# Six layers of local attention on one core: which projections stand next to each other in a slot, and how the other engines' orders follow

## What is computed

```python
qkv = shift_tokens(x) @ Wqkv            # 128 x 128 times 128 x 3072
q, k, v = split(qkv, 3)                 # 16 heads of 64 each
q, k = l2norm(q) * qs, l2norm(k) * ks   # norms over each head
q = q * cos * scale + rotate_half(q) * sin * scale     # k with 1 / scale
sim = 8 * q @ k.T                       # windows of 32, looking one window back
out = softmax(mask(sim)) @ v
x = out @ Wo + x
```

## Time and profile before

| | us |
|---|---|
| median of 3 runs (1913.93 to 1918.66) | 1914.29 |
| the profiled execution, its own time | 1919.0 |
| its span, first to last instruction | 1916.2 |

### The profile page before, as it was taken

How to read it: one execution, slowest core, us unless ns; L and a number is a source line. 1 busy time by engine, 2 the same in 40 slices (tenths; PEclk the granted TensorE clock), 3 DMA queues, 4 the chain that set the end, 5 groups by cost and what they waited for, 6 DMA issues and landing times.

```text
span 1916.2 us, 85177 instructions
## 1 busy us (share of the span) xinstructions
PE 1742.9 (91%) x33584; PEld 1377.8 (72%) x33584; DVE 1613.1 (84%) x3868; ACT 1389.4 (73%) x3701; POOL 1331.6 (69%) x1226
## 2 busy tenths in 40 slices
PE   5888869999899999899998899998999998999997
PEld 3444447787777787777787777787787776787776
DVE  6666679999679999589998699996799995899985
ACT  4677657877677877577886677885777875777875
POOL 4444457888478888388887488885688874888882
PEclk9899879999999999999999999999999999999999
DMA  5000011111021111021111211111211110211111
GB/s 130 5 5 4 2 59 42 33 38 40 24 74 41 33 40 39 23 75 40 33 37 32 67 41 40 33 37 31 68 43 38 33 43 20 76 40 39 33 36 48
DMA packets 59087, 77.46 MB, mean 40 GB/s; under 512 B 16608, under 2 KB 31674, under 8 KB 57914
## 3 DMA queue, kind: packets, MB, share of 16 engines
q1 hardware_dynamic: 58938, 75.36, 15.1%
HBM read 22.63 MB, written 1.05 MB: 12 GB/s over the span
## 4 chain that ended last, share of the span: by engine, by line
PE 59%; DVE 14%; ACT 9%; POOL 8%; issue 8%; SPq 1%; DMA 0%; POOLq 0%; DVEq 0%; ACTq 0%
PE y_ps L524 9%; PE s_ps L476 7%; PE proj_ps L455 7%; PE tr_ps L465 6%; POOL qk L1519 5%; PE pv_ps L506 4%; PE proj_ps L457 4%; PE proj_ps L456 4%; ACT square L818 4%; DVE by_cos L1091 3%; PE s_ps L698 3%; DVE by_sin L1091 3%; DVE sumsq L1103 3%; PE y_ps L516 2%; PE proj_ps L684 2%
## 5 line engine op out<-in xcount | busy, mean ns | idle before, releaser
L1512 POOL TENSOR_TENSOR qk<-by_cos,by_sin 128x512 f32<-128x512 f32 x388 | 498.4, 1285 | 199.1 <-DVE by_sin L1091 198.0
L1519 POOL TENSOR_TENSOR qk<-qk,inv_norm 128x512 f32<-128x512 f32 x388 | 404.4, 1043 | 82.2 <-ACT inv_norm L824 67.9
L818 ACT ACTIVATE square<-proj_ps 128x512 f32<-128x512 f32 x364 | 217.6, 598 | 110.0 <-PE proj_ps L457 92.9
L455 PE MATMUL proj_ps<-w_hi,x_hi 128*128 128x512 f32 x546 | 268.2, 491 | 22.9 <-DVE by_sin L1091 20.3
L1091 DVE TENSOR_TENSOR by_cos<-proj_ps,tab 128x512 f32<-128x512 f32 x364 | 249.9, 687 | 34.4 <-ACT square L818 32.5
L465 PE MATMUL tr_ps<-ident,qk 128*128 128x128 f32 x1544 | 238.7, 277 | 40.2 <-POOL qk L1519 25.5
L1103 DVE TENSOR_REDUCE sumsq<-square 128x8 f32<-128x512 f32 x388 | 262.3, 676 | 0.0
L465 PEld LDWEIGHTS tr_ps<-ident,qk 128*128 128x128 f32 x1544 | 181.1, 142 | 110.3 <-POOL qk L1519 79.1
L1091 DVE TENSOR_TENSOR by_sin<-proj_ps,tab 128x512 f32<-128x512 f32 x364 | 247.8, 681 | 0.0
L1525 POOL TENSOR_TENSOR s_sb<-s_sb,row_max 128x512 f32<-128x512 f32 x192 | 205.0, 1068 | 32.5 <-DVE row_max L1122 31.7
L457 PE MATMUL proj_ps<-w_hi,x_lo 128*128 128x512 f32 x546 | 217.1, 398 | 0.0
(11 more groups left out here) (173 smaller groups left out, 4160.5 us busy)
## 6 DMA issues: line engine op xcount, KB each, us to landing
arena<-v SPq DMA_DIRECT2D x388, 130.0 KB, 2.4
w_raw<-in_L_ffn_Wqkv SPq DMA_DIRECT2D x7, 1536.0 KB, 6.8
wo<-in_L_ffn_Wo SPq DMA_DIRECT2D x7, 512.0 KB, 3.9
w_raw<-in_L_ffn_W SPq DMA_DIRECT2D x7, 341.0 KB, 6.2
c_in<-in_ctx SPq DMA_DIRECT2D x16, 64.0 KB, 1.8
xn<-in_fside_BxS SPq DMA_DIRECT2D x1, 1024.0 KB, 6.1
out<-z SPq DMA_DIRECT2D x4, 256.0 KB, 2.9
w<-in_L_ffn_W SPq DMA_DIRECT2D x12, 64.0 KB
```

The source lines that it names most:

```text
L455: pe.matmul(ps[:], x_hi[:], w_hi[:, col], start=True, stop=False)
L818: act.activation(square[:, c % 2, :], ps[QK_AT[c] % 2][:], ACT.Square).then_inc(squared, 1)
L1512: pool.tensor_tensor(heads(qk[:, c, :]), heads(by_cos[:, c % 2, :]), heads(by_sin[:, c % 2, :])[:, :, ::-1, :], ALU.add).then_inc(qk_added, 1)
L1519: pool.tensor_tensor(ap, ap, inv_norm[:, c, :].unsqueeze(2).to_broadcast([128, 8, DH]), ALU.mult).then_inc(qk_ready, 1)
```

## The change

Only the order of calls within a slot changes, on PE, ACT, DVE and POOL. No instruction is added or removed. The core of the diff, in the order PE, ACT, DVE, POOL:

```diff
                     if front_on:
                         project(T + 1, 0)
+                        project(T + 1, 1)
                     if behind >= 1:
                         p_transpose(T - 1, 1)
-                    if front_on:
-                        project(T + 1, 1)
+                    if behind >= 2:
+                        shift_state(T - 2, tile_of(z, n - 2, D // 2))
                     if first:
                         qk_transpose(T, 2)
                     qk_transpose(T, 3)
-                    if behind >= 2:
-                        shift_state(T - 2, tile_of(z, n - 2, D // 2))
                     if behind >= 1:
                         values(T - 1, 1 - par, 1)
-                    if front_on:
-                        project(T + 1, 2)
-                    if behind >= 1:
-                        att_transpose(T - 1, 0)
                     scores(T, par, 1)
...
+                    if behind >= 1:
+                        att_transpose(T - 1, 0)
                     if front_on:
+                        project(T + 1, 2)
                         project(T + 1, 3)
+                        project(T + 1, 4)
                         qk_transpose(T + 1, 0)
+                    p_transpose(T, 0)
                     if behind >= 1:
                         att_transpose(T - 1, 1)
-                    p_transpose(T, 0)
                     if front_on:
-                        project(T + 1, 4)
                         qk_transpose(T + 1, 1)
                         project(T + 1, 5)
...
-                    if front_on:
-                        square_chunk(T + 1, 1)
                     if first:
                         qk_out(T, par, 2)
                     qk_out(T, par, 3)
                     if front_on:
+                        square_chunk(T + 1, 1)
                         norms(T + 1, 0)
-                    if behind >= 1:
-                        att_out(T - 1, 0)
-                    if front_on:
-                        v_out(T + 1, 1 - par, 0)
                     exps(T, 0)
...
                     if front_on:
+                        v_out(T + 1, 1 - par, 0)
+                        norms(T + 1, 1)
                         square_chunk(T + 1, 2)
-                        norms(T + 1, 1)
+                    if behind >= 1:
+                        att_out(T - 1, 0)
...
                     if behind >= 1:
                         sums_inverse(T - 1, 1)
+                        normalise(T - 1, 1)
                     if behind >= 2:
                         dve.wait_ge(stat_done, T - 1)
-                    if behind >= 1:
-                        normalise(T - 1, 1)
+                    if front_on and not last_front:
+                        stage(T + 2, n + 2, L * 4 + 12)
                     if behind >= 2:
                         ln_variance(T - 2, par)
                     if front_on:
-                        clamp_norm(T + 1, 1)
+                        times_cos(T + 1, 2, L - 1)
+                        times_sin(T + 1, 2, L - 1)
+                        sum_squares(T + 1, 2)
                     mask(T, 1)
...
-                    if front_on:
-                        sum_squares(T + 1, 2)
-                    if front_on and not last_front:
-                        stage(T + 2, n + 2, L * 4 + 12)
-                    if front_on:
-                        clamp_norm(T + 1, 2)
-                    if behind >= 2:
-                        ln_apply(T - 2, n - 2, par)
+                    sums_inverse(T, 0)
+                    normalise(T, 0)
                     if front_on:
                         times_cos(T + 1, 3, L - 1)
                         sum_squares(T + 1, 3)
+                        clamp_norm(T + 1, 3)
                         times_sin(T + 1, 3, L - 1)
-                        clamp_norm(T + 1, 3)
-                    sums_inverse(T, 0)
-                    normalise(T, 0)
+                    if behind >= 2:
+                        ln_apply(T - 2, n - 2, par)
...
                         add_rotated(T + 1, 2)
+                        scale_rotated(T + 1, 2)
                     center(T, 1)
                     if not front_on:
                         w_rest(1, L * 3 + 2)
-                    if front_on:
-                        scale_rotated(T + 1, 2)
```

More of the change, by code:

```diff
@@ L999, in slot @@
                     if front_on:
+                        v_out(T + 1, 1 - par, 0)
+                        norms(T + 1, 1)
                         square_chunk(T + 1, 2)
-                        norms(T + 1, 1)
+                    if behind >= 1:
+                        att_out(T - 1, 0)
+                    if front_on:
                         qk_out(T + 1, 1 - par, 0)
+                    p_out(T, 0)
                     if behind >= 1:
@@ L1006, in slot @@
                         ln_std(T - 2, par)
-                    p_out(T, 0)
                     if front_on:
                         qk_out(T + 1, 1 - par, 1)
+                        norms(T + 1, 2)
                         square_chunk(T + 1, 3)
-                        norms(T + 1, 2)
                     if front_on and not last_front:
@@ L1015, in slot @@
                         v_out(T + 1, 1 - par, 1)
+                        qk_out(T + 1, 1 - par, 2)
                     exps(T, 1)
-                    if front_on:
-                        qk_out(T + 1, 1 - par, 2)
                 layer_slots(act.Fori, L, slot)
@@ L1383, in slot @@
                         times_sin(T + 1, 0, L - 1)
-                        clamp_norm(T + 1, 0)
                     if behind >= 2:
@@ L1387, in slot @@
                     if front_on:
+                        clamp_norm(T + 1, 0)
                         times_cos(T + 1, 1, L - 1)
@@ L1390, in slot @@
                         sum_squares(T + 1, 1)
+                        clamp_norm(T + 1, 1)
                     if behind >= 1:
                         sums_inverse(T - 1, 1)
+                        normalise(T - 1, 1)
                     if behind >= 2:
                         dve.wait_ge(stat_done, T - 1)
-                    if behind >= 1:
-                        normalise(T - 1, 1)
+                    if front_on and not last_front:
+                        stage(T + 2, n + 2, L * 4 + 12)
                     if behind >= 2:
@@ L1404, in slot @@
                     if front_on:
-                        times_cos(T + 1, 2, L - 1)
-                        times_sin(T + 1, 2, L - 1)
+                        clamp_norm(T + 1, 2)
                     row_maxima(T, 1)
```

## The result

The changed kernel takes 1969.51 us (median of 4 runs, 1965.38 to 1975.19) against 1916.47 (4 runs, 1913.93 to 1918.81), a ratio of 1.0279 with a 95% interval of 1.0257 to 1.03. It is slower by about 53 us. The profiled executions have spans of 1973.4 and 1916.2, 57.2 apart.

What follows compares the result with a forecast made beforehand. DVE, with 13.92 us of work in a 14.41 us slot, was to bound: +0.32 +0.12 +0.37 +0.12 gives 14.85, above PE's 14.06. Over 78 slots that is 34 us, less 2, so 1946 us (own range 1925 to 1970, widened to begin at 1893).

Steps and rivals of the forecast that it cites:

- The sum of the slot: DVE's work per slot: 13.92 us now plus four terms, 14.85 us after the change.
- Term 1: DVE's ln_apply, moved behind times_sin of chunk 3, stands behind POOL's add: 1.44 us against 1.12, +0.32 per slot.
- The rival in which it gets through: ln_apply's second half asks before POOL's add and costs 0.39 us; PE's 14.06 then bounds, 1885 us; chance 0.18.
- Term 2: DVE's staging, moved behind normalise of T - 1, stands behind POOL's add of chunk 1: 0.47 us against 0.35, +0.12.
- Term 3: DVE's clamps of chunks 1 and 3 wait for their own sums of squares: +0.37 us per slot in all.
- Term 4: DVE's sums_inverse of half 0, now ahead of chunk 3's rotation, waits for the late values: +0.12 us per slot.
- The step of PE's neighbours: Three of six projections per slot directly follow another, first matmul 0.39 us instead of 0.50: 0.3 us saved on PE.
- The size in microseconds: 0.44 us more in each of 78 slots, 34 us, less 2 for slots 0 and 1: 1914.3 + 32 = 1946.

Runs made afterwards that it cites:

- e3: The changed kernel with ln_apply directly behind normalise of half 0, in front of the whole rotation of chunk 3; the slot is longer by 0.60 us.
- e10: The kernel before with projection 1 directly behind projection 0 on PE and p_transpose behind both; 1924.5 us.
- e7: The kernel before with POOL's center of half 1 held back until ln_apply is done; slower by 0.3 to 0.7%.
- e12: The changed kernel without the second half of ln_apply, so part of the result is not computed; 1918.9 us, slot 14.20 us.
- e11: The changed kernel with project 2 on PE between the values of T - 1 and the scores of half 1; 1954.6 us.
- e8: The changed kernel with PE's order of the kernel before, other engines keeping their changed orders; 2048 us.
- e1: The changed kernel with POOL's add_rotated of chunk 3 waiting until ln_apply is done; 0.12 us of the time saved on DVE reaches the slot.
- e2: The changed kernel with ln_apply moved in front of times_sin of chunk 3; 0.18 us of the time saved on DVE reaches the slot.
- e4: The kernel before with ln_apply alone moved behind times_sin of chunk 3; slower by 0.63 us per slot, 49 us in 78.
- e9: The changed kernel with chunk 3's rotation before sums_inverse and normalise, ln_apply before its times_sin, and POOL's center of half 1 waiting for ln_apply; slot 15.15 us.
- e5: The changed kernel with POOL's add_rotated of chunk 3 waiting for ln_apply and ACT's square of chunk 1 at its old place; slot 14.74 us.

## Why the prediction was right, and what it missed

**The sum of the slot held.** Forecast 14.85 us, measured 14.86.

- Term 1: `ln_apply` costs 955.36 - 953.91 = 1.45, forecast 1.44, with the first half through in 0.27 and the second standing, 0.03 us behind POOL, as the earlier trace rows had it. (At 483.85 in those rows the second half lasted 1.07; it did not lose 1.07, as the prediction says. Nothing hangs on that.) By the Trainium skill (SBUF — State Buffer, Who interferes with whom) whoever issues first holds the shared pair for the whole instruction; the traces agree at margins of 0.03 and 0.04 us (954.07 and 954.10 here, 954.04 and 954.08 in e3). The rival in which it gets through is refuted for this place.
- Term 2: the staging takes 0.61 (947.09 to 947.70) and 0.58 in the other slot of the body (961.99 to 962.57), forecast 0.47. +0.25 instead of +0.12. DVE reaches it 3.89 us behind `times_sin` of chunk 0 (943.20), not 4.03, and POOL's add ends 4.49 behind it (forecast 4.50), so it stands longer.
- Term 3: the clamps were too dear. Two now wait for their sum (0.71 behind its start at 945.45 against 0.60), 0.11 each, 0.22 where 0.37 stood.
- Term 4: the wait for the values is 951.06 - 950.27 - 0.60 = 0.19, forecast 0.12.
- Together 0.33 + 0.25 + 0.17 + 0.19 = 0.94, and 13.92 + 0.94 = 14.86. The 0.17 for the clamps is what the other three leave; counted directly it is 0.2. Errors of 0.1 in both directions cancelled.

**The step of PE's neighbours held in size and bought nothing.** Two of three pairs have the short first matmul, the third waits 0.27 for its bank. e10 shows the pair alone at no gain.

**What failed is the picture of the limits behind the sum.** The prediction took a slot for the larger of two amounts, DVE's own work and PE's own sequence. It said that in the kernel before DVE "carries 13.92 us of work in a slot of 14.41", and for the changed kernel it set DVE's 14.85 against PE's 14.06. But the chain of the kernel before is a loop over PE, ACT, DVE and POOL of 14.41 us with 1.89 us of DVE in it, and e7, which took 0.73 us off DVE, gained nothing. That DVE's work and this loop are nearly of one length is chance, and it let the forecast from DVE's work come out. In the changed kernel, too, the chain leaves DVE in each slot: from the rotation of chunk 0 over POOL (944.04) to PE's transposes (948.87) and values, and back to `sums_inverse` at 951.06, where DVE waits 0.19. Term 4 had this wait as 0.12 us of DVE's time, not as the closing of a loop. The rival "The second half gets through" gave 14.06 us and 1885. e12, the nearest to it, gave 14.20 and 1918.9: 0.14 us in 78 slots are 11 us, and slots 0 to 3 and 14 are 17 us longer than before (446.3 against 429.5).

**The size in microseconds was short by 23 us** (1946 against 1969.5). The result lies 0.5 us inside the upper end of the range, and two of its four executions lie above 1970; that it is inside is luck. The step is "so many slots times the difference, 2 us less for slots 0 and 1, nothing for the rest". The 60 slots 4 to 13 gave 29.1, near the forecast (60 x 0.44 = 26). The 30 others gave 30.6, where the prediction had 18 x 0.44 - 2 = 6. Slots 0 and 1 were forecast 2 us shorter and came out 11.4 longer, 3.7 of it without any stall; why these two are slower without `ln_apply`, no run shows. e11 shows that the place of the scores directly behind the values, 64 small matmuls in a row (its expectation counts 96, by the records of the one and the matmuls of the other), causes a large part: project 2 between them takes 15 us off. e8, with PE's old order, has no more stalls than before. That PE is short of instructions there is the reading that fits (small matmuls in a row, code run for the first time); the profile shows only that it waits for nothing else. Why e11 keeps 5.0 us, and what makes the clock fall behind one stall and not behind another, stays open.

**Is the stall the cause of the 53 us?** Of the longer slot, yes. e12 leaves out the stalled half, and the slot falls from 14.86 to 14.20, below the 14.38 of before. e1 and e2 look as if they spoke against it, since the changed kernel still loses 45 us in them; but they buy the missing stall by delaying POOL's add, and the loop of 14.7 us that then holds them has this delay in it. The remaining part, some 18 us, is PE's stalls and what follows them in the slots outside the pattern, and e12 still has it: it gains 11 us against before in the 60 slots 4 to 13 (851.9 against 862.7) and loses 17 in the 30 others. In the kernel before, moving `ln_apply` alone (e4) costs 48 us, by the stall and the lost cover together. No experiment gave a kernel faster than before.

## What to carry to other kernels

- A busy share near the slot's length on one engine doesn't show that this engine binds. Follow the chain of the profile once around a slot and add up the pieces to the slot's length; then look for the second loop before pricing what the first one's removal gives.
- The same stalled instruction is free in front of a wait and counts in full behind it. Moving a step out of such cover costs the cover, whatever else it brings (e4, e9).
- Neighbouring matmuls of one kind save 0.1 us each on PE; what was moved from between them comes later for those who wait for it (0.37 us in e10, and no gain). And the small matmuls that then become neighbours had stalls of up to 2.1 us in code that runs for the first time.
- A probe that takes a stall away by a new wait has the new wait in its result. Ask which loop that wait lengthens before reading the result as the price of the stall (e1, e5, e7).

## Hardware behaviour that I had not expected

- PE stalls of 0.6 to 2.3 us that wait for nothing shown, mostly within the small matmuls of the scores: 9.5 to 12.2 us in all at the scores in the eight kernels in whose PE order the values and the scores are neighbours, the changed one among them, and 1.8 to 5.0 in the other six, the kernel before among them. Behind four of the eight in the changed kernel the granted clock fell to 0.50, the lower of the two levels, 1.2 instead of 2.4 GHz; behind the one at 1719.91 matmuls stood 0.42 instead of 0.23 us apart.
- A DVE instruction of 0.28 us lasts 1.33 if it starts 0.03 us behind the start of a POOL instruction of 1.28, and POOL's own length doesn't change (mean 1.285 in both kernels). A DVE instruction during which POOL starts loses little or nothing: the first half takes 0.27 where POOL starts 0.16 us into it (953.91 and 954.07), and 0.36 in e4 where POOL starts 0.23 us into it (931.87 and 932.10).
